# Multi-query attention on one core: the score products of the first two query tiles packed into shared banks

## The reference, cut to what matters

```
Q = (x @ Wq + bq).reshape(B, S, H, Dh)          # H = 16, Dh = 8
K = x @ Wk + bk ; V = x @ Wv + bv               # one head for all
A = einsum('bhqd,bkd->bhqk', Q, K)
A = where(causal, A, -inf)
P = softmax(A / sqrt(Dh), axis=-1)
O = einsum('bhqk,bkd->bhqd', P, V) ; return O @ Wo + bo
```

## Time and profile before

| | |
|---|---|
| median of 3 runs | 3526.26 us (3525.94 to 3530.38) |
| the profiled execution | 3527.43 us, span 3525.7 us |
| mean granted TensorE clock | 0.984 |
| scores of the first layer written | 21.3 to 375.2 us |
| maxima (L741) | x512, 27.8 to 375.5 us |

### The profile page before, as it was taken

One profiled execution on the slowest core, in us unless ns is written; L12 is line 12 of the kernel. 1 busy time (PEld: TensorE's weight loads), 2 busy tenths in 40 slices (PEclk: granted clock), 3 DMA queues, 4 the chain that ended last, 5 costly groups with the idle time before them and its releaser, 6 DMA issues. The chain is left out here.

```text
span 3525.7 us, 158966 instructions
## 1 busy us (share of the span) xinstructions
PE 3299.0 (94%) x66105; PEld 2780.2 (79%) x66106; DVE 2967.9 (84%) x4613; ACT 2693.1 (76%) x4132; POOL 2599.2 (74%) x3334
## 2 busy tenths in 40 slices
PE   7999579999999999999999999999999999999984
PEld 5677358888788888788887888887888887888874
DVE  6777568888888888988889888889888888888864
ACT  4777458888788888788888888888888887888862
POOL 5677477778777777777777777777777787777762
PEclk9999899999999999999999999999999999999997
DMA  2000023222223222232222232222232222222221
GB/s 59 5 7 7 16 62 93 65 71 71 63 74 89 67 71 71 68 94 64 67 71 71 67 94 64 68 71 68 69 95 64 68 71 74 64 70 64 69 62 60
DMA packets 161734, 228.08 MB, mean 65 GB/s; under 512 B 42265, under 2 KB 60641, under 8 KB 161505
## 3 DMA queue, kind: packets, MB, share of 16 engines
q1 hardware_dynamic: 161632, 226.85, 24.0%
HBM read 21.00 MB, written 4.19 MB: 7 GB/s over the span
## 5 line engine op out<-in xcount | busy, mean ns | idle before, releaser
L1175 POOL TENSOR_TENSOR by_cos<-by_cos,by_sin 128x1024 f32<-128x1024 f32 x384 | 911.4, 2385 | 14.9 <-DVE by_sin L1529 14.9
L1181 POOL TENSOR_TENSOR by_cos<-by_cos,norms 128x1024 f32<-128x1024 f32 x384 | 734.5, 1913 | 13.0
L1527 DVE TENSOR_TENSOR by_cos<-proj,turns 128x1024 f32<-128x1024 f32 x384 | 470.1, 1224 | 185.8 <-ACT squares L1417 159.4
L1261 PE MATMUL proj<-qkv_hi,xs_hib 128*128 128x512 f32 x1152 | 512.6, 445 | 48.2 <-DVE by_sin L1529 39.2
L1529 DVE TENSOR_TENSOR by_sin<-proj,turns 128x1024 f32<-128x1024 f32 x384 | 466.1, 1214 | 0.0
L1533 DVE TENSOR_REDUCE sumsb<-squares 128x16 f32<-128x1024 f32 x384 | 464.5, 1210 | 1.5 <-DVE w_lo L1596 1.5
L1417 ACT ACTIVATE squares<-proj 128x1024 f32<-128x1024 f32 x384 | 393.3, 1024 | 86.9 <-PE proj L1263 86.1
L1263 PE MATMUL proj<-qkv_hi,xs_lob 128*128 128x512 f32 x1152 | 459.0, 398 | 0.0
L1262 PE MATMUL proj<-qkv_lo,xs_hib 128*128 128x512 f32 x1152 | 458.0, 398 | 0.0
L1270 PE MATMUL ring<-ident,by_cos 128*128 128x128 f32 x3072 | 386.2, 274 | 8.2 <-DVE xT L1630 4.9
L1397 ACT ACTIVATE vb<-proj 128x1024 f32<-128x1024 f32 x192 | 195.2, 1017 | 256.3 <-DMA v_win<-vb 212.7
(11 more groups left out here) (190 smaller groups left out, 7888.1 us busy)
## 6 DMA issues: line engine op xcount, KB each, us to landing
v_win<-vb SPq DMA_DIRECT2D x1152, 128.0 KB, 2.3
v_win<-vb SPq DMA_DIRECT2D x768, 64.0 KB, 2.0
in_qkv<-L_ffn_Wqkv SPq DMA_DIRECT2D x12, 768.0 KB
wo<-L_ffn_Wo SPq DMA_DIRECT2D x6, 512.0 KB, 4.1
x_tok<-L_attn_x SPq DMA_DIRECT2D x8, 256.0 KB, 3.9
residual<-x_tok SPq DMA_DIRECT2D x8, 256.0 KB, 2.0
o_x<-residual SPq DMA_DIRECT2D x1, 2048.0 KB, 9.3
out<-o_x SPq DMA_DIRECT2D x8, 256.0 KB, 2.2
```

What stands on the lines that cost most here:

```text
L1175: nc.gpsimd.tensor_tensor(both, both, by_sin[:, j, :], ALU.add).then_inc(e[f"{w_}_added"].sem, 1)
L1181: nc.gpsimd.tensor_tensor(heads, heads, inverse, ALU.mult).then_inc(e[f"{w_}_ready"].sem, 1)
L1261: nc.tensor.matmul(out, xs_hi[:, tile], qkv_hi[:, cols], start=True, stop=False)
L1527: nc.vector.tensor_tensor(of_heads(by_cos[:, t % 2, j, :]), heads, table(0), ALU.mult)
```

## The change

The queries of tile 1 of two heads share a product of 2 x 256 columns and one bank, and those of tile 0 of all four heads of a group share a product of 4 x 128 columns and one bank. The moving operand is a view of the keys' copies of two or four heads. A group then has 11 fills in place of 12: tile 3 and tile 2 of each head, and as third fill the pair of heads 0 and 1 at head 0, the four of tile 0 at head 1, the pair of heads 2 and 3 at head 2, and none at head 3. Tile 2 has its bank alone. VectorE takes one maximum per head and tile as before, in the order of the fills, and counts a bank once. Waits for keys are widened to the heads that share a product.

```
@@ -81,7 +81,7 @@
 HEADS = B * MQA_H
 QKV_W = D + 2 * MQA_D
 SCORE_SCALE = float(np.float32(1.0) / np.sqrt(np.float32(MQA_D)))
-FILLS = 3
+GROUP_FILLS = 11
 QUERIES_AT = (8, 11, 12, 15)
 SUM_STATISTICS_AT = (6, 8, 9, 10)
 
@@ -114,7 +114,10 @@
 
     if not 0 <= m < HEADS:
         return ()
-    return (3, FILLS * m), (2, FILLS * m + 1), (1, FILLS * m + 2)
+    group, i = m // PER_GROUP, m % PER_GROUP
+    first = GROUP_FILLS * group + 3 * i
+    shared = {0: ((1, first + 2),), 1: ((0, first + 2),), 2: ((1, first + 2),), 3: ()}[i]
+    return ((3, first), (2, first + 1), *shared)
 
 
 def mqa_stage(nc, c, semaphore, weights, x_in, credits, arrived, residual, first_layer):
@@ -130,7 +133,7 @@
 
         x_tok, xT = c["x_tok"], c["xT"]
         ident, ident_bf, ones = c["ident"], c["ident_bf"], c["ones"]
-        mask_qk, masked = sb("a_mask_qk", [P, S]), sb("a_masked", [P, FILLS * S])
+        mask_qk, masked = sb("a_mask_qk", [P, S]), sb("a_masked", [P, 3 * S])
         wqkv = sb("a_wqkv", [P, QKV_W])
         wo = sb("a_wo", [P, D])
         bias_in, bias_hi = sb("a_bias_in", [2, QKV_W + D]), sb("a_bias_hi", [2, QKV_W + D], F32R)
@@ -295,7 +298,7 @@
             def negated_maxima(group):
                 b, g = group // GROUPS, group % GROUPS
                 heads = slice(g * PER_GROUP, (g + 1) * PER_GROUP)
-                pool.wait_ge(s_max, PER_GROUP * FILLS * (group + 1))
+                pool.wait_ge(s_max, GROUP_FILLS * (group + 1))
                 pool.wait_ge(q_full, group + 1)
                 nc.gpsimd.tensor_scalar(qa[b % 2][:, :, heads, 24], row_max[:, :, heads], -1.0, None,
                                         ALU.mult).then_inc(m_hi, 1)
@@ -380,13 +383,17 @@
                 if qt == 3:
                     if i == 0:
                         pe.wait_ge(q_done, GROUPS * b + g + 1)
-                    pe.wait_ge(keys_done, PER_GROUP * b + i + 1)
+                    pe.wait_ge(keys_done, PER_GROUP * b + min(i + 2, PER_GROUP))
                     last = nc.tensor.matmul(out[:, :], queries(3), keys[:, i, :], start=True, stop=True)
                 elif qt == 2:
-                    nc.tensor.matmul(out[:, 0:3 * P], queries(2), keys[:, i, 0:3 * P], start=True, stop=True)
-                    last = nc.tensor.matmul(out[:, 3 * P:4 * P], queries(0), keys[:, i, 0:P], start=True, stop=True)
+                    last = nc.tensor.matmul(out[:, 0:3 * P], queries(2), keys[:, i, 0:3 * P], start=True, stop=True)
+                elif qt == 1:
+                    last = nc.tensor.matmul(out[:, :].rearrange("p (h k) -> p h k", h=2), queries(1),
+                                            keys[:, i:i + 2, 0:2 * P], start=True, stop=True)
                 else:
-                    last = nc.tensor.matmul(out[:, 0:2 * P], queries(1), keys[:, i, 0:2 * P], start=True, stop=True)
+                    pe.wait_ge(keys_done, PER_GROUP * b + PER_GROUP)
+                    last = nc.tensor.matmul(out[:, :].rearrange("p (h k) -> p h k", h=PER_GROUP), queries(0),
+                                            keys[:, :, 0:P], start=True, stop=True)
                 last.then_inc(s_full, 1)
 
             def scoresT(n, k):
@@ -565,7 +572,7 @@
 
             def queries_turned(b, g):
                 act.wait_ge(q_full, GROUPS * b + g + 1)
-                at_least(act, s_full, PER_GROUP * FILLS * (GROUPS * (b - 1) + g + 1))
+                at_least(act, s_full, GROUP_FILLS * (GROUPS * (b - 1) + g + 1))
                 copy(qT0[:, g, :], near[:, :]).then_inc(q_done, 1)
 
             def turned_with_max(group):
@@ -733,18 +740,24 @@
             def maxima(m, qt, fill):
                 h = m % MQA_H
                 dve.wait_ge(s_full, fill + 1)
-                at_least(dve, s_max, fill - FILLS + 1)
-
-                def largest(qt, at):
+                at_least(dve, s_max, fill - 2)
+
+                def largest(h, at):
                     n = (qt + 1) * P
-                    place = slice((fill % FILLS) * S + at, (fill % FILLS) * S + at + n)
+                    place = slice((fill % 3) * S + at, (fill % 3) * S + at + n)
                     return nc.vector.tensor_tensor_reduce(
                         out=masked[:, place], in0=score[fill % 2][:, at:at + n], in1=mask_qk[:, 4 * P - n:4 * P], scale=1.0,
                         scalar=LOWEST, op0=ALU.add, op1=ALU.max, accum_out=row_max[:, qt, h:h + 1])
 
-                last = largest(qt, 0)
-                if qt == 2:
-                    last = largest(0, 3 * P)
+                if qt >= 2:
+                    last = largest(h, 0)
+                elif qt == 1:
+                    largest(h, 0)
+                    last = largest(h + 1, 2 * P)
+                else:
+                    group = h - h % PER_GROUP
+                    for k in range(PER_GROUP):
+                        last = largest(group + k, k * P)
                 last.then_inc(s_max, 1)
 
             def weighted(group):
```

More of the change, by code:

```diff
@@ L382, in scores @@
                         pe.wait_ge(q_done, GROUPS * b + g + 1)
-                    pe.wait_ge(keys_done, PER_GROUP * b + i + 1)
+                    pe.wait_ge(keys_done, PER_GROUP * b + min(i + 2, PER_GROUP))
                     last = nc.tensor.matmul(out[:, :], queries(3), keys[:, i, :], start=True, stop=True)
                 elif qt == 2:
-                    nc.tensor.matmul(out[:, 0:3 * P], queries(2), keys[:, i, 0:3 * P], start=True, stop=True)
-                    last = nc.tensor.matmul(out[:, 3 * P:4 * P], queries(0), keys[:, i, 0:P], start=True, stop=True)
-                else:
-                    last = nc.tensor.matmul(out[:, 0:2 * P], queries(1), keys[:, i, 0:2 * P], start=True, stop=True)
+                    last = nc.tensor.matmul(out[:, 0:3 * P], queries(2), keys[:, i, 0:3 * P], start=True, stop=True)
+                elif qt == 1:
+                    last = nc.tensor.matmul(out[:, :].rearrange("p (h k) -> p h k", h=2), queries(1),
+                                            keys[:, i:i + 2, 0:2 * P], start=True, stop=True)
+                else:
+                    pe.wait_ge(keys_done, PER_GROUP * b + PER_GROUP)
+                    last = nc.tensor.matmul(out[:, :].rearrange("p (h k) -> p h k", h=PER_GROUP), queries(0),
+                                            keys[:, :, 0:P], start=True, stop=True)
                 last.then_inc(s_full, 1)
```

## The result

The kernel after takes 3548.62 us, median of 4 runs (3544.89 to 3552.25), against 3526.86 (4 runs, 3525.94 to 3530.38) before: a ratio of 1.0061, 95% interval 1.0049 to 1.0074, so 22 us slower. The forecast was 3551.3 in a range of 3540 to 3561.

What follows compares the result with a forecast made beforehand. TensorE's stream paced the first layer, with VectorE's release of score banks just in time; 21.6 us over six full batches, +2.1 and -1 in the first, +2.1 and +0.3 in the last summed to +25, so 3551.3 us, range 3540 to 3561.

Steps and rivals of the forecast that it cites:

- The loop of the bank: Next load of a shared score bank waits for VectorE's maxima, 1.26 us after a two-head product, 1.40 after a four-head one.
- The six full batches: First-layer batches of 16 heads: each 3.6 us longer than 44.5, in sum 21.6 us.
- The cover: Steps h = 8 to 10: TensorE's 0.5 us delay hides behind a 0.81 us wait for GpSimd, so costs nothing.
- The stream: TensorE's products per group of four heads: 0.72 us goes, 0.69 comes, a 512-column product costing 0.23; nearly nothing.
- no stall: Rival: the bank's next load isn't held by VectorE; only 0.2 us per group changes, -6.5, 3520 us; chance 0.03.
- a price per product: Rival on TensorE: three 512-column products cost 0.12 us each like a small one, no stall; -17, 3509 us; chance 0.02.
- The covered case: Rival: TensorE's stall eats other waits; cost falls to 1 to 2 us a batch, +7 to +14, 3537; chance 0.08.
- The clock case: Rival: longer waits bring a dip to the lower clock in six more batches, 1.7 us each; +10, 3561; chance 0.07.
- the start: First batch's first steps, VectorE-bound: shorter second fills close a 0.24 us gap in up to ten steps; -1 taken (0 to -2.4).
- the first batch: Steps 5 to 7 and 11 to 15 like other batches, +2.1 us; its clock dip vanishing would give back 1.7.
- the last batch: First layer's final batch: h = 0 to 7 +2.1 us, h = 8 to 10 +0.3, nothing after, no scores left.

## Why the prediction was right

**The loop of the bank.** Right in place and size: 1.25 and 1.42 us from the product to the next load of the bank against 1.26 and 1.40, behind 12 products a batch. The step lengths, after less before, in the fifth batch (h counted from the 512-column product of one step to that of the next, so that neighbouring steps share a term):

```
h       0     1     2     3     4     5     6     7     8     9     10    11    12    13    14    15
us    +0.61 -0.15 +0.02 +0.40 +0.61 +0.17 +0.03 +0.40 +0.55 -0.15 -0.40 +0.39 +0.54 +0.17 +0.01 +0.41
```

Sum +3.61; forecast 3.6. Term by term, with the forecast in brackets: h = 3, 7, 11 and 15 are 0.39 to 0.41 each (0.40); h = 12 0.54 (0.55); h = 4 0.61 (0.60); h = 0 0.61 (0.60); h = 1 and 2 together -0.13 (0.10 - 0.22); h = 5 and 6 +0.20 and h = 13 and 14 +0.18 (each 0.40 - 0.22); h = 8 to 10 together 0.00 (0). The six full batches from the second on came to 21.2 together (21.6).

**The cover.** The 0.81 us wait for GpSimd fell to 0.39 in the batch after:

```profile
262.36 0.66 PE L374 MATMUL a_near<-ident,a_qa 128*128 128x128 f32 x4 [0.39 <-POOL a_qa L306]
```

and with the key spreads out of the way the steps cost 0.4 more. "Cost: nothing; if the cover were gone, 0.5 a batch" held.

**The stream.** The rivals "no stall" and "a price per product" are out: 8 us below the kernel before when the drain is short, but 22 above with it. (What the prediction said for "no stall", that no wait view names L386, holds for the batch only: over the whole kernel before, L386 waits 4 times for a row maximum, 0.9 us in all.) The trace has 0.23 us from one 512-column product to the next, in the kernel after too. The Trainium skill, "TensorE: Matmul & The Clock Gate", section "Back-to-back issue gap", has 131 ns there for a sustained stream of weight loads and products; the measurement decides against it here. The gap of about 216 ns that the same section gives for a single product of N=512 is nearer.

**The covered case** is out by the batch: no further wait was eaten. **The clock case** is out: the granted clock is 1.00 in the batch after, with 5.1 us of waits at L389 in it.

**What was mis-sized.** First, the start. "Shorter second fills close it in up to ten steps: between 0 and -2.4, I take -1" was wrong in sign. The transposed scores begin at 42.3 us in place of 39.4, and the first five steps take 0.9 longer. The first score product starts 1.5 later (22.8 in place of 21.3), since it now waits for two key spreads, which the prediction had looked at for h = 10 only. But that costs nothing: the third fill starts at 28.59, before the change at 28.56. The 2.9 come behind it, where the loads of tile 2 wait four times for a shared bank, 0.39 to 0.60 us each:

```profile
22.79 0.76 PE L387 MATMUL a_score<-a_kT,a_qT 128*128 128x512 f32 x1 [2.13 <-POOL a_kT L285]
...
33.24 0.69 PE L389 MATMUL a_score<-a_kT,a_qT 128*128 128x384 f32 x1 [0.60 <-DVE a_row_max L748]
```

With one maximum per bank the transposed scores begin at 38.9, with two maxima in the kernel before at 42.4: the start thus follows the hold of the bank, and the prediction had looked only at the second fill.

Second, the first batch: its wait at h = 10 fell, and no clock dip follows (1.00; 0.57 in the earlier trace rows). That gave 1.5 us back (the step h = 11 is 1.2 shorter, where it is 0.4 longer in a later batch), which the prediction named and did not count.

```profile
71.56 0.65 PE L374 MATMUL a_near<-ident,a_qa 128*128 128x128 f32 x4 [1.66 <-POOL a_qa L306]
...
68.00:76.00 8.00, 6.01 (x47) 4.59 (x46) 3.90 (x19) 5.01 (x11) 6.47 (x11) 1.00 0.00 0
76.00:84.00 8.00, 7.59 (x59) 4.78 (x60) 4.99 (x21) 5.18 (x12) 4.96 (x12) 1.00 0.00 1
```

Third, the later layers: the sum took every gain and loss to be in the first. There it measured +26.5 in the profiled run, forecast +25; the later layers gave back some of it, and the median came out at +22. Term by term, the start and the first batch came to +4.0 (+1.1 forecast), the six full batches to +21.2 (+21.6), the last batch to +1.3 (+2.4). So the batch was understood, and that the total came within 3 us of the forecast is in part luck: the start and the first batch were 2.9 too low in it, and the last batch and the later layers made up for that.

## What to carry to other kernels

Ahead of packing more work into a PSUM bank, follow the bank, not the products: product end, reader's start, all of its readers, release, next load. If that loop has no slack (here TensorE already waited 0.04 us), nearly all the time of each reader added to the bank is paid by TensorE (0.34 or 0.35 us a step for a reader of 0.35), though VectorE is idle a quarter of the time; if the wide bank is put where TensorE has other work before it needs it again, most of it isn't. A loss that is covered by another wait comes back when that wait is mended. And a difference of some microseconds between two versions should be looked for in the changed stage of the trace first, since 128 empty waits moved this kernel by 6.

## What the runs showed of the hardware that was not expected

- With 128 waits and no work added at the head of TensorE's queue the later, unchanged layers were 8 us shorter (3102.0 to 3093.8; the median of the kernel 6), with a granted clock of 1.00 and 0.93 in place of 0.93 and 0.92 in two windows near the end.
- Two maxima on one bank follow each other in 0.35 us (256 columns) or 0.21 (128), though each is recorded as 0.42 and 0.28: the next starts with the read-out of the one before. The hold of a bank is a sum of these spacings, to 0.02 us.
- From a product's recorded end to VectorE's start 0.03 to 0.04 us, from a read-out's end to the waiting load 0.05 to 0.06, in the timelines of all the kernels here.
